# Loading x three steps ahead into freed parking rows, and one class gather a step, in a two-layer conditioned residual kernel

## The reference

```python
U = (mu @ W_dec + b_dec).reshape(B, 513, 30)
param = jnp.einsum('bik,kj->bij', U, V)
x = x + jnp.einsum('bsd,bde->bse', x, param[:, :-1]) + param[:, -1][:, None]
h = _ln(x, pw_g[pathway_ids], pw_b[pathway_ids])      # 500 rows
h = _ln(h, cp_g[compartment_ids], cp_b[compartment_ids])   # 5 rows
t = _ln(x, tm_g[compartment_ids], tm_b[compartment_ids])   # 5 rows, the same ids
s = _ln(x, ms_g[mask], ms_b[mask])                    # 3 rows, the mask is 0 or 1
m, n, r = (x + _mlp_ln(state_k, ...) for each of three condition vectors)
cat = concatenate([w[0]*h, w[1]*t, w[2]*m, w[3]*n, w[4]*r, w[5]*s])
x = x + _ln(silu(cat @ int_W1 + int_b1) @ int_W2 + int_b2, int_g, int_be)
```

## Time and profile before

| | |
|---|---|
| median of 3 runs | 638.94 us (632.1, 638.94, 640.89) |
| the profiled execution | 633.35 us, of which the trace's span is 631.5 us |
| PE busy | 593.8 us, 94% of the span |
| DVE, ACT, POOL busy | 406.9 us (64%), 205.4 us (33%), 388.2 us (61%) |
| granted PE clock, mean | 0.991 of full speed |
| DMA | 102.07 MB, 162 GB/s over the span; queue q1 (SP) 58.52 MB, q0 (POOL) 42.04 MB |
| chain that ended last | PE 67%, issue 8%, DMA 8%, POOL 7%, DVE 6%; the line with `DMA sgt<-in_ms_g,idx` has 3% |

### The profile page before, as it was taken

One profiled execution on the slowest core, in us unless ns is written; L12 is line 12 of the kernel. 1 busy time (PEld: TensorE's weight loads), 2 busy tenths in 40 slices (PEclk: granted clock), 3 DMA queues, 4 the chain that ended last, 5 costly groups with the idle time before them and its releaser, 6 DMA issues.

```text
span 631.5 us, 9140 instructions
## 1 busy us (share of the span) xinstructions
PE 593.8 (94%) x2924; PEld 456.1 (72%) x2924; DVE 406.9 (64%) x749; ACT 205.4 (33%) x346; POOL 388.2 (61%) x499
## 2 busy tenths in 40 slices
PE   0899978989999999999999999999999999999995
PEld 0455536457888888888888877877888888788784
DVE  3411256568888888888775566655666575576754
ACT  3333433242344333343232323322233222323222
POOL 1002454676888888888766656677776676676720
PEclk9999978999999999999999999999999999999999
DMA  8999987413554454455433444443433344344301
GB/s 293 404 404 386 344 280 247 130 57 115 154 174 139 148 162 139 145 169 166 129 115 106 138 111 133 138 135 107 146 114 125 113 132 120 121 135 124 100 18 50
DMA packets 53119, 102.07 MB, mean 162 GB/s; under 512 B 10446, under 2 KB 23246, under 8 KB 52956
## 3 DMA queue, kind: packets, MB, share of 16 engines
q1 hardware_dynamic: 39872, 58.52, 26.9%
q0 software_dynamic: 12160, 42.04, 22.1%
q10 hardware_dynamic: 1052, 1.07, 0.5%
HBM read 93.10 MB, written 8.39 MB: 161 GB/s over the span
## 4 chain that ended last, share of the span: by engine, by line
PE 67%; issue 8%; DMA 8%; POOL 7%; DVE 6%; ACT 2%; SPq 1%; POOLq 0%; DVEq 0%
PE bank L707 18%; PE bank L708 17%; PE bank L709 17%; PE bank L701 7%; DMA ring<-in_W_dec 4%; DMA sgt<-in_ms_g,idx 3%; PE bank L758 2%; DVE bn L1213 2%; PE bank L695 2%; POOL rs L993 1%; SPq L319 1%; POOL h L1045 1%; POOL h L1043 1%; PE bank L777 1%; POOL ctt L1010 1%
## 5 line engine op out<-in xcount | busy, mean ns | idle before, releaser
L707 PE MATMUL bank<-W,ops 128*128 128x512 f32 x432 | 179.1, 415 | 0.4
L708 PE MATMUL bank<-W,ops 128*128 128x512 f32 x432 | 171.9, 398 | 0.0
L709 PE MATMUL bank<-W,ops 128*128 128x512 f32 x432 | 171.8, 398 | 0.0
L555 ACT ACTIVATE ops<-bank 128x512 fp32r<-128x512 f32 x97 | 57.0, 589 | 139.2 <-PE bank L701 139.2
L707 PEld LDWEIGHTS bank<-W,ops 128*128 128x128 f32 x432 | 82.0, 190 | 26.9 <-issue 8.5
L709 PEld LDWEIGHTS bank<-W,ops 128*128 128x128 f32 x432 | 82.0, 190 | 20.1
L708 PEld LDWEIGHTS bank<-W,ops 128*128 128x128 f32 x432 | 82.1, 190 | 15.1
L1034 POOL TENSOR_TENSOR xop<-xraw,xop 128x512 fp32r<-128x512 f32 x32 | 42.7, 1335 | 65.9 <-ACT xop L526 65.8
L1208 DVE TENSOR_TENSOR ops<-bank,ops 128x512 fp32r<-128x512 f32 x97 | 66.3, 684 | 13.3 <-ACT ops L555 13.1
L1213 DVE BATCH_NORM_STATS2 bn<-h 128x6 f32<-128x512 f32 x32 | 22.2, 693 | 72.1 <-POOL h L1045 72.1
L985 POOL TENSOR_SCALAR ve<-mv 128x1 f32<-128x1 f32 x94 | 31.5, 336 | 37.3 <-DVE mv L1217 33.4
(11 more groups left out here) (143 smaller groups left out, 1072.2 us busy)
## 6 DMA issues: line engine op xcount, KB each, us to landing
ring<-in_W_dec SPq DMA_DIRECT2D x16, 960.0 KB, 12.1
xraw<-in_xT SPq DMA_DIRECT2D x32, 256.0 KB, 4.8
x<-in_x SPq DMA_DIRECT2D x32, 256.0 KB
out<-xb SPq DMA_DIRECT2D x31, 256.0 KB, 2.0
ring<-in_int_W SPq DMA_DIRECT2D x4, 1024.0 KB, 8.8
mnr<-in_int_W SPq DMA_DIRECT2D x12, 256.0 KB, 8.1
stash<-in_xT SPq DMA_DIRECT2D x12, 256.0 KB, 11.7
idxrep<-in_rows SPq DMA_DIRECT2D x64, 32.0 KB
```

What stands on the lines that cost most here:

```text
L555: nc.scalar.activation(dst.rearrange("p c t -> p (c t)"), bank[:, :], ACT.Copy).then_inc(done, 1)
L707: nc.tensor.matmul(bank[:, :], op[:, HI, c, :], w[:, HI, c, :], start=start and c == 0, stop=False)
L708: nc.tensor.matmul(bank[:, :], op[:, HI, c, :], w[:, LO, c, :], start=False, stop=False)
L709: last = nc.tensor.matmul(bank[:, :], op[:, LO, c, :], w[:, HI, c, :], start=False, stop=stop and c == KC - 1)
```

## The change

1. x is loaded three steps ahead. The four `stash` rows 0 to 3 serve again as a ring once their parked results are used (`z_whole`): for tile 14 and later (`ringed`), transposed x goes into row s mod 4. The load waits for POOL's `x_low` of the tile four before, no longer for PE. ACT's `x_high` now waits itself until PE has freed `xop` (`x_free`). Parked tiles still load into `xraw`.
2. The two gathers `ctt` and `sgt` become one, `cls`, of 6 KB a token, from a table of 15 rows (5 compartments x 3 scales). A fourth integer beside each token's three is its row number, 3 x compartment + scale; DVE works it out in `class_row`, after `out_stats`, and POOL's gather waits for that (`row_ready`). `st` and `tt` read `cls`.
3. The class numbers are loaded three steps ahead too, into a ring of four; the first four come in one load on ACT's queue, and DVE makes their row numbers in one instruction in the prologue.
4. On POOL `residual` of f moves ahead of the gather of `pwt`. On SP the x load of a parked tile stands ahead of `load_rows` throughout.

```diff
+def ringed(t):
+    return t.exists() and not kept(t) and t.s >= PRE0 + NPRE
...
-        idx = sb("idx", [P, 2, 3], I32)
+        idx = sb("idx", [P, UNROLL, 4], I32)
-        ctt = sb("ctt", [P, 2, 2 * D])
-        sgt = sb("sgt", [P, 2, D])
+        cls = sb("cls", [P, 2, 3 * D])
...
+        def x_rows(a):
+            return stash[:, a.row, :]... if ringed(a) else xraw[a.slot][:, :, :]
...
+            def load_ahead(a):
+                s, old, pair = a.slot, a.plus(-UNROLL), a.pair()
+                if ringed(old):
+                    sp.wait_ge(x_lo, old.count())
+                else:
+                    sp.wait_ge(z_whole, a.row + 1)
+                sp.dma_start(x_rows(a), d["xT"][...]).then_inc(stash_in[a.row], 16)
+            def load_index(a):
+                s, old, pair = a.slot, a.plus(-UNROLL), a.pair()
+                read = old.slot_count(16)
+                if old.exists():
+                    sp.wait_ge(ct_in[s], read)
+                    sp.wait_ge(pw_in[s], read)
+                sp.dma_start(idx[:, a.row, 0:3], d["idx"][...]).then_inc(idx_in[s], 16)
...
             def load_rows(a):
...
-                    sp.wait_ge(sg_in[s], done)
-                    sp.wait_ge(ct_in[s], done)
-                    sp.wait_ge(pw_in[s], done)
-                sp.dma_start(idx[:, s, :], d["idx"][...]).then_inc(idx_in[s], 16)
...
             def step(n):                                   # SP
-                a, done = n.plus(2), n.plus(-3)
+                a, ahead, done = n.plus(2), n.plus(3), n.plus(-3)
                 if done.exists():
                     store(done)
+                if kept(a):
+                    load_x(a)
                 if a.exists():
-                    if kept(n):
-                        load_x(a)
                     load_rows(a)
-                    if not kept(n):
-                        load_x(a)
+                if ahead.exists():
+                    if not done.exists():
+                        sp.wait_ge(row_ready, UNROLL)
+                    load_index(ahead)
+                if ringed(ahead):
+                    load_ahead(ahead)
...
+            load(act, first_idx_in, (idx[:, :, 0:3], d["first_idx"]))
...
             def x_high(a):
+                old = a.plus(-2)
+                if ringed(a):
+                    act.wait_ge(stash_in[a.row], ring_count(a))
+                    if kept(old):
+                        act.wait_ge(xu_ready, old.count())
+                    else:
+                        act.wait_ge(x_free, old.count())
+                else:
+                    act.wait_ge(xT_in[s], a.slot_count(16))
...
             def gather_class(a):
-                pool.wait_ge(idx_in[s], a.slot_count(16))
+                pool.wait_ge(row_ready, a.count())
...
-                gather(a, ctt, "ct", 1, ct_in)
+                gather(a, cls, "cls", 3, ct_in)
             def gather_rest(a):
-                gather(a, sgt, "ms_g", 2, sg_in)
                 gather(a, pwt, "pw", 0, pw_in)
...
                     rstd(1, f, mv2_ready, r2_ready)        # POOL step
+                    residual(f)
                 if a.exists():
                     gather_rest(a)
-                if f.exists():
-                    residual(f)
...
+            v.wait_ge(first_idx_in, 16)                    # DVE prologue, after lm_ready
+            nc.vector.scalar_tensor_tensor(out=idx[:, :, 3:4], in0=idx[:, :, 1:2], scalar=3.0, in1=idx[:, :, 2:3],
+                                           op0=ALU.mult, op1=ALU.add).then_inc(row_ready, UNROLL)
...
+            def class_row(a):
+                v.wait_ge(idx_in[a.slot], a.slot_count(16) - 16 * UNROLL // 2)
+                nc.vector.scalar_tensor_tensor(out=idx[:, a.row, 3:4], in0=idx[:, a.row, 1:2], scalar=3.0,
+                                               in1=idx[:, a.row, 2:3],
+                                               op0=ALU.mult, op1=ALU.add).then_inc(row_ready, 1)
...
                 out_stats(b)                               # DVE step
+                if a.exists():
+                    class_row(a)
                 if f.exists():
                     scale_rows(f)
```

More of the change, by code:

```diff
@@ L248, in build, with ring_count @@
         V4, wlast = stash[:, NPRE - 1, :], stash[:, NPRE - 2, 0:2 * P].rearrange("p (c r) -> p c r", r=P)
+        def x_rows(a):
+            return stash[:, a.row, :].rearrange("p (c t) -> p c t", t=P) if ringed(a) else xraw[a.slot][:, :, :]
+        def ring_count(a):
+            return a.row_count(16) - 16 * ((PRE0 + NPRE + UNROLL - 1 - a.row) // UNROLL - 1)
         def z_op(c):
@@ L269, in build @@
         ring_in = [sem(f"ring_in{i}") for i in range(SLOTS)]
-        pre_in = [sem(f"pre_in{p}") for p in range(NPRE)]
+        stash_in = [sem(f"stash_in{p}") for p in range(NPRE)]
         pre_hi, pre_lo, pre_used, pre_stash = sem("pre_hi"), sem("pre_lo"), sem("pre_used"), sem("pre_stash")
@@ L383, in load_pre @@
                     sp.wait_ge(ulast_ready, 1)
-                load(sp, pre_in[p], (pre_rows(p), d["xT"][t.batch, t.pair(), :, :, :]))
+                load(sp, stash_in[p], (pre_rows(p), d["xT"][t.batch, t.pair(), :, :, :]))
             def load_x(a):
@@ L393, in load_x @@
                     "o p c t -> (o p) c t")).then_inc(xT_in[s], 16)
+            def load_ahead(a):
[4 more added lines that the diff above has]
+                    sp.wait_ge(z_whole, a.row + 1)
+                sp.dma_start(x_rows(a), d["xT"][s, bass.ds(pair, 1), :, :, :].rearrange(
+                    "o p c t -> (o p) c t")).then_inc(stash_in[a.row], 16)
+            def load_index(a):
[4 more added lines that the diff above has]
+                    sp.wait_ge(pw_in[s], read)
+                sp.dma_start(idx[:, a.row, 0:3], d["idx"][s, bass.ds(pair, 1), :, :].rearrange("o p n -> (o p) n")) \
+                  .then_inc(idx_in[s], 16)
             def load_rows(a):
                 s, old, pair = a.slot, a.plus(-2), a.pair()
-                done, read = old.slot_count(16), old.count()
+                read = old.count()
                 if old.exists():
@@ L508, in pre_high @@
             def pre_high(p):
[L509 removed]
+                act.wait_ge(stash_in[p], 16)
                 if p >= 2:
@@ L1010, in gather @@
                 pool.indirect_dma_start(out=dst[:, s, :], out_offset=None, in_=d[table],
-                                        in_offset=bass.IndirectOffsetOnAxis(ap=idx[:, s, col:col + 1], axis=0)) \
+                                        in_offset=bass.IndirectOffsetOnAxis(ap=idx[:, a.row, col:col + 1], axis=0)) \
                     .then_inc(got[s], 16)
@@ L1251, in scaled @@
                     v.wait_ge(tT, m.count())
-                nc.vector.tensor_tensor(tt[:, :], xhat[:, :], ctt[:, s, D:2 * D], ALU.mult).then_inc(t_ready, 1)
+                nc.vector.tensor_tensor(tt[:, :], xhat[:, :], cls[:, s, D:2 * D], ALU.mult).then_inc(t_ready, 1)
             def scale_rows(f):
@@ L1256, in scale_rows @@
                 v.wait_ge(xhat_ready, f.count())
-                v.wait_ge(sg_in[s], f.slot_count(16))
+                v.wait_ge(ct_in[s], f.slot_count(16))
                 if m.exists():
                     v.wait_ge(sT, m.count())
-                nc.vector.tensor_tensor(st[:, :], xhat[:, :], sgt[:, s, :], ALU.mult).then_inc(s_ready, 1)
+                nc.vector.tensor_tensor(st[:, :], xhat[:, :], cls[:, s, 2 * D:3 * D], ALU.mult).then_inc(s_ready, 1)
             def h_stats(f):
@@ L1268, in h_gain @@
                 v.wait_ge(hn_ready, f.count())
-                nc.vector.tensor_tensor(ht[:, :], ht[:, :], ctt[:, f.slot, 0:D], ALU.mult).then_inc(h_ready, 1)
+                nc.vector.tensor_tensor(ht[:, :], ht[:, :], cls[:, f.slot, 0:D], ALU.mult).then_inc(h_ready, 1)
             def t_split(m):
@@ L1536 @@
         "idx": np.stack([path, comp, scale], axis=-1),
+        "first_idx": np.stack([np.stack([v[s % B, s // B] for v in (path, comp, scale)], axis=-1) for s in range(UNROLL)],
+                              axis=1),
         "rows": np.stack([scale, comp], axis=1),
@@ L1547 @@
         "pw": np.concatenate([L1["pw_g"], L1["pw_b"]], axis=1),
-        "ct": np.concatenate([L1["cp_g"], L1["tm_g"]], axis=1),
-        "ms_g": L1["ms_g"],
+        "cls": np.concatenate([np.repeat(np.concatenate([L1["cp_g"], L1["tm_g"]], axis=1), 3, axis=0),
+                               np.tile(L1["ms_g"], (5, 1))], axis=1),
         "int_W1": L1["int_W1"], "int_W2": L1["int_W2"],
```

10 lines of the change are left out of this document (3 added, 7 removed).

## The result

| | before | after |
|---|---|---|
| median of 22 runs each | 632.96 us (629.55 to 640.89) | 638.17 us (635.64 to 640.27) |
| ratio after to before | | 1.0074, 95% interval 1.0053 to 1.0095 |
| the profiled execution, its span | 633.35, 631.5 us | 638.97, 637.2 us |
| DVE, POOL busy | 406.9, 388.2 us | 436.8, 368.4 us |

The change makes the kernel 0.7% slower. That is within the 2% called no change, but it is a loss, and the forecast was a gain. A line number of the kernel after is another than before: L773 is now L809, L1269 (`ht`) is L1312, L1260 (`st`) is L1303, L1054 (`residual`) is L1089, L1034 (`x_low`) is L1069, the gathers' line is L1046.

A forecast was written before the change was run, and what follows sets the result against it. PE, busy 94%, was taken as the bound. Span 631.5 minus 5.8 in the full steps plus 0.3, with 1.85 around it, gave 627.9; the middle between that and 633.4 was 630.5 us, range 625.5 to 637.5.

The forecast's parts named there:

- The row number on DVE: Parked steps: `class_row` delays `st` by 0.1 to 0.25 us, covered by 0.6 us of slack; bounds 0 to 0.5, taken as 0.
- neither DVE nor POOL holds PE back there: Parked steps: PE takes 14.15 us a step and is not held back by either engine.
- Given back in the parked steps: Rival: port and row-number wait use up the 0.6 us slack; 11 steps x 0.5 = 5.5 us back, 636; chance 0.11.
- `residual` ahead of the gathers: POOL: `residual`, 1.32 us, takes the `sgt` gather's place, so the `pwt` gather is issued within 0.1 us of before.
- The port rule: Parked steps: `class_row` waits for `x_low`'s end and pushes the gather by its own length; 0.1 to 0.3 us of slack used.
- The 18 full steps: Full steps after the parked ones: 5.8 us of loss from waits for x and `sgt` ends, 0.3 us left there.
- the new waits on SP: SP queue: the waits of `load_ahead` and `load_index` are for work done long before, so they cost nothing.
- Another transfer: Rival, full steps: x now goes out with other transfers, `pwt` ends last, half the loss stays; 633.4; chance 0.10.
- Slower: Rival, class gather: a 6 KB row landing later than 13.8 us makes `st` wait; 2% loss at about 14.8; chance 0.04.
- the prologue stayed: Prologue: extra load and three fewer gathers cost and win nothing; bounds 4.1 us won to 1 us lost, taken as 0.
- The base: Profiled execution, 633.35 us, was 5.6 us below the median of 638.94; the middle of 627.9 and 633.4 was taken.

The follow-up runs named there:

- e9: e5 with `class_row` put back in the change's place behind `out_stats`: 635.29 us, ratio 1.0046 to before.
- e6: Before, with the statistics of x taken twice in parked steps, the second result unused: 638.8 us, ratio 1.01 to before.
- e4: Before, with only `residual` moved ahead of the `sgt` and `pwt` gathers: timed runs 632.04, 635.47, 1191.39 and 2070.0 us, no ratio.
- e5: After, with `class_row` behind `x_stats`, and `residual` behind the gathers and waiting for `ht`: 627.05 us, ratio 0.9907 to before.
- e11: Before, with an unused 128x1 DVE instruction at `class_row`'s place in parked steps, alternately with two SBUF inputs and one: 628.53 us, one run.
- e7: Before, with only the x loads of tile 14 and later three steps ahead (point 1): 627.96 us, ratio 0.9925 to before.
- e8: e5 with x loaded as before the change: 628.43 us, ratio 0.9919 to before.
- e3: After, with both `class_row` moved behind `x_stats` and `residual` put back behind the gathers: 663.86 us, ratio 1.0501 to before.
- e1: After, with only `residual` put back behind the gathers on POOL: 671.33 us, ratio 1.064 to before.
- e2: After, with only `class_row` moved on DVE to behind `x_stats`: 634.31 us, ratio 1.0064 to before.
- e10: e9 with `class_row` at the same place working out the row of the next step's tile: 636.79 us, ratio 1.0102 to before.

## Why the prediction was wrong

630.5 us was forecast, 625.5 to 637.5 the range; measured are 638.17 us. By its steps:

- **The failed step** is in "The row number on DVE": "The cover is the slack at the end: `ht` ends at 269.95 and PE takes it at 270.55, 0.6 us", and with it "I take 0". The 0.6 us is a lead that can be used up once, not in each step; what a step has to spare is 0.07 us. e9 shows the lead gone and 0.6 us lost in most steps, and e6 that 0.6 us added to the ring costs 0.55 us a step. The neighbouring `ht` rows would have shown it before any run. For the same reason "neither DVE nor POOL holds PE back there" was true and no argument: the two together come round in 14.05 us.
- **The rival "Given back in the parked steps"** had the mechanism, the place and nearly the time (636). Its 0.5 us was about 1.0: the gather's 0.67, and 0.33 in `ht`, which the prediction did not have at all. Its "Against it", that parked steps held PE's pace with `st` blocked already, was the failed step again, and is why it had a chance of only 0.11.
- **`residual` ahead of the gathers** was costed at nothing. I looked only at what it did to the gather of `pwt`, not at which DVE instruction would run beside it. In the change that was `ht`, 0.33 us a step (after against e9). In before the same move would have cost 7.9 us (e4), as there it falls on the cast: its price hangs on what stands beside it.
- **The port rule** was weighed and drawn too small: "push the gather by its own length", 0.1 to 0.3 us. That `class_row` waits for the end of `x_low` was right. But it ends there within 0.02 us, and the gather starts 0.81 us later in place of 0.16: 0.67 lost by POOL's wait, of which the instruction's length is no part. No row stood for the price of such a wait.
- **The 18 full steps** went as forecast (16.9 to 17.0 us, no wait for x or for a gather) and gave 4.4 us by the two profiled executions, not 5.5: the first one carries the ring's lateness over, 17.90 us. In e5, where the ring is not late, it is 314.95 - 298.01 = 16.94 and the gain is 5.4. Some luck is in both, as before's 310.37 was 1.6 to 1.9 more than the same steps took in e6 and e11. Which of its two causes was removed is another matter: e7, e8 and e4 show that any one of three edits ends the loss.
- **Right**: the new waits on SP cost nothing, `cls` lands with 9 us to spare (rivals "Another transfer" and "Slower" are out), the prologue stayed.
- **The base.** I put half of the 5.6 us between the profiled execution and the median of three down to removable waits. Over 22 runs before has 632.96 us, so the profiled execution was an ordinary one, and there was nothing to explain. The forecast against that base would have been 632.96 - 5.5 = 627.5; the 10.7 us missed are the 10.1 of the parked steps and 1.1 of the first full one, less half a us unaccounted for.

That the ring sets the parked steps, and that `class_row`'s wait and `residual`'s place add to it, is shown by e5, e6, e9 and after against e9. Still open: what POOL does in the 0.81 us behind its wait for the row number; by what path moving `residual` (e4) takes the loop's wait for x away, and the x ring (e7) that for `sgt`.

## What to carry to other kernels

An engine's lead of x us over its consumer, the same in every step, is cover once, not in each step: take the period of the chain that feeds it (the same instruction in two successive steps) and compare it with the consumer's period; only the difference is cover. Before placing a POOL instruction, list the DVE instructions with two SBUF inputs, and the casts, that will run beside it, the shortest included, and ask which chain waits for these. Here one wait, for `ht` before `residual`, made 5.9% of difference between e3 and e5. The gain of 0.9% that is left is hardly more than either half of the change brings alone (0.75% and 0.8%), and under the 2% called no change.

## What the runs showed of the hardware

- A DVE instruction on 128x1 with two SBUF inputs took 0.57 us beside a POOL tensor operation and 0.12 with one input. The Trainium skill ("SBUF — State Buffer", Who interferes with whom) has just this distinction, and the trace agrees. It ended 0.01 to 0.02 us after POOL's instruction, so its time is what is left of that one. A 128x512 one ended 0.54 to 0.57 us after.
- The same section of the Trainium skill says, of the two-port modes, that the one that issues first holds the pair. For two-input instructions the starts in the profile don't bear that out here: `ht` of e1 started at 411.22 and `residual` at 411.74, L1371 of after at 240.49 and L1078 at 240.89, and both DVE instructions ended 0.56 to 0.57 us after POOL's. Each began while POOL was still issuing a gather; but `ht` of e5 began beside such an issue too and took 0.69. So the start shown is not the moment at which it is decided.
- The cast of 128x128 from SBUF to SBUF, with one input, took 1.30 to 1.38 us when it started with `residual` (e2, e4) and 0.23 in the parked steps of before. So one input alone does not keep an instruction clear of POOL.
- A gather whose row number DVE finished as POOL's `x_low` ended started 0.81 us later, and one that waited for no row number 0.14 to 0.17 us after `x_low` (after and e9 against e5, e10 and e11).
- The issue of a gather takes POOL 0.9 to 1.3 us whether its rows have 2, 4 or 6 KB.
